# Turning the router's matmul around in two sorted expert stages: the weights stand still, the rows move, and the logits are turned back

## The chip, the core and the metric

The kernel runs on one core of a Trainium2 chip. The metric is the device time in microseconds (us) of one execution, the median of several. TensorE (PE, and PEld for its weight loads) has two clock levels, 1.2 and 2.4 GHz; the profile gives the granted level of a stretch as 0.50 or 1.00.

## The reference, cut to what matters

A stack of eight layers works on `x` (8 batches of 256 rows of 256 numbers). Two of them are mixtures of experts, each of which first computes logits of a router for every row, then picks two experts for a row from them:

```python
# layer 0: 16 experts
scores = xf @ gate_w.T
scores = jax.nn.softmax(scores.astype(jnp.float32), axis=-1)
...
_, idx = jax.lax.top_k(scores, TOPK)
# layer 1: 8 experts
logits = jnp.einsum('bsd,de->bse', x, gate_w) + gate_b
scores = jax.nn.softmax(logits, axis=-1)
topk_s, topk_i = jax.lax.top_k(scores, K)
```

Here `xf` and `x` are the layer's normalised rows: 2048 rows of 256. The router's weights are 256 x 16 in layer 0 and 256 x 8 in layer 1.

## The kernel before, in words

The program is a list of stages, `a0, f0, a1, f1, a2, f2, a3, f3`; each is a block of its own, and no engine begins a stage before all have ended the one ahead (the sequencer rows of L143 are that seam). The stages of interest are `f0` (`sorted_gated_experts`, E = 16) and `f1` (`sorted_experts`, E = 8). Both start in the same way.

VectorE normalises the 16 tiles of 128 rows (L2340 in f0, L2690 in f1) and tells TensorE after every second tile, that is after every batch b. TensorE turns a batch with four transposes of 128 x 128 (`transpose_xn`, L329) into one of two PSUM banks `GP`. ScalarE copies the turned batch to `xnT` in SBUF (L2200, L2616), which later matmuls need too. One step behind, TensorE computes the logits of the batch (L2252, L2649): for each of its 2 tiles and each of the 2 halves of the 256 features, a tile of `xnT` (128 x 128) is loaded as the stationary side and the router's weights, 16 or 8 columns, move:

```python
for t in range((b - 1) * TT, b * TT):
    for k in range(KD):
        op = pe.matmul(logits[:, t * E:(t + 1) * E], xnT[:, k, t * P:(t + 1) * P], wr[:, k, :],
                       start=(k == 0), stop=(k == KD - 1))
```

A float32 matmul of the program stands in the trace as two matmuls with two weight loads, a transpose as one of each; so a batch has 8 pairs for its logits and 4 for its transposes. The logits of all 16 tiles come to lie in one PSUM bank, rows on the partitions (`LG` in f0, `YB[0]` in f1).

When the last is in, `logits_full` lets VectorE go on (L2348 in f0, L2697 in f1): softmax with one exponential on ScalarE (L2202, L2618), the choice of two experts, counts of rows for each expert (two matmuls on TensorE, L2279 and L2280 in f0, L2656 and L2657 in f1), and from these the place of each row in a table sorted by expert. GpSimd then scatters the rows to DRAM with indirect DMAs (L2187, 32 of them; L2603, 16), SyncE fetches them back tile by tile (L2171, L2592), and TensorE starts on the experts (L2298, L2663). In f0 TensorE, ScalarE, GpSimd and VectorE also compute shared experts for all rows meanwhile (L2262 and L2269, L2208 to L2214, L2135 and L2138), in a loop over batches. SyncE zeroes the table (L2162, L2580) and, in f0, loads all experts' weights (L2165) behind that.

Of the kernel before, what the change touches and what calls it, by code (L numbers as in the profile page):

```python
# [17 lines left out]
ACT = mybir.ActivationFunctionType  # L18
AX = mybir.AxisListType

P = 128
B, S, D = 8, 256, 256
TT = S // P
KD = D // P
# [330 lines left out]
def at_least(eng, sem, count):  # L355
    if count > 0:
        eng.wait_ge(sem, count)
# [1688 lines left out]
def sorted_gated_experts(nc, g, name, w):  # L2046
# [9 lines left out]
    E, G, SH = 16, 4, 2  # L2056
# [5 lines left out]
    with ExitStack() as ctx:  # L2062
        sb = lambda n, s, t=F32: ctx.enter_context(nc.sbuf_tensor(f"{name}_sb_{n}", s, t))
        sems, from_one = [], []

        def sem(n, one=False):

            s = ctx.enter_context(nc.semaphore(f"{name}_{n}"))
            (from_one if one else sems).append(s)
            return s  # L2070
        x_slots = nc.dram_tensor(f"{name}_x_slots", (NS * P, D), F32).ap()
        y_slots = g.y_slots[0] = nc.dram_tensor(f"{name}_y_slots", (NS * P, D), F32).ap()
        wr, br = sb("wr", [P, KD, E]), sb("br", [P, E])
# [12 lines left out]
        xnT = sb("xnT", [P, KD, B * S])  # L2086
# [13 lines left out]
        s_y = sb("s_y", [P, TT, D])  # L2100
# [3 lines left out]
        ps = lambda n: ctx.enter_context(nc.psum_tensor(f"{name}_{n}", [P, 2, S], F32))  # L2104
        GP, HB, YB = [ps("gp0"), ps("gp1")], [ps("hb0"), ps("hb1")], [ps("yb0"), ps("yb1")]
        HT = LG, CT = ps("lg"), ps("ct")

        router_in, shared_in, experts_in = sem("router_in"), sem("shared_in"), sem("experts_in")
        sqrt_in, sqrt_out, fixed, cleared = sem("sqrt_in"), sem("sqrt_out"), sem("fixed"), sem("cleared")
        xn_ready, xn_turned, xnT_ready = sem("xn_ready"), sem("xn_turned"), sem("xnT_ready")  # L2110
        logits_full, shifted, exp_ready = sem("logits_full"), sem("shifted"), sem("exp_ready")
        both_ready, counted, routed = sem("both_ready"), sem("counted"), sem("routed")
        s_full = [sem(f"s_full{e}") for e in range(SH)]
# [81 lines left out]
        @block.scalar  # L2195
        def _(act):
            norm_sqrt(act, g, sqrt_in, sqrt_out)
            for b in range(B):
                act.wait_ge(xn_turned, b + 1)
                act.activation(xnT[:, :, b * S:(b + 1) * S], GP[b % 2][:], ACT.Copy).then_inc(xnT_ready, 1)  # L2200
            act.wait_ge(shifted, 1)
            act.activation(ex[:], lg[:], ACT.Exp).then_inc(exp_ready, 1)  # L2202
            act.wait_ge(shared_in, 16 * 5)
            with act.Fori(0, B) as b:
                for e in range(SH):
                    act.wait_ge(s_full[e], b + 1)
                    act.wait_ge(s_product[e], b + 1)
                    act.activation(s_act[:, e], HB[e][:, 0], ACT.Silu, bias=bs1[:, e:e + 1])  # L2208
                    act.activation(s_lin[:, e], HB[e][:, 1], ACT.Identity, bias=bs3[:, e:e + 1])\
                       .then_inc(s_evacuated[e], 1)  # L2210
                act.wait_ge(s_y_full, b + 2)
                act.wait_ge(s_y_added, b + 1)
                for t in range(TT):
                    op = act.activation(s_y[:, t], YB[t][:, 0], ACT.Copy)  # L2214
                op.then_inc(s_y_copied, 1)

            def work(first, last):
                for what, p in slot_steps(first, last):
                    q = p % PAIRS
                    if what == "turn":  # L2220
                        act.wait_ge(turned[q], nth(p))
                        act.activation(xsT[:, ring(p)], GP[p % 2][:], ACT.Copy).then_inc(xT_ready[q], 1)
                    elif what == "hidden":
                        act.wait_ge(h_biased[q], nth(p))
                        act.activation(hm[:, ring(p)], hb[:, ring(p), 0:P], ACT.Silu).then_inc(h_act[q], 1)
                    elif what == "turn_h":
                        act.wait_ge(hT_full[q], nth(p))
                        act.activation(hmT[:, ring(p)], HT[p % 2][:, 0, :].rearrange("p (j n) -> p j n", n=P), ACT.Copy)\
                           .then_inc(hT_ready[q], 1)
                    elif what == "out":  # L2230
                        act.wait_ge(y_ready[q], nth(p))
                        act.dma_start(slots(y_slots, p), ys[:, ring(p), :]).then_inc(y_stored[q], 16)

            work(0, ALWAYS)
            with last_turn(act):
                work(ALWAYS, ALL)

        @block.tensor
        def _(pe):
            pe.wait_ge(router_in, 16 * 6)  # L2240
            logits = LG[:].rearrange("p a n -> p (a n)")
            for b in range(B + 1):
                if b < B:
                    pe.wait_ge(xn_ready, b + 1)
                    if b >= 2:
                        pe.wait_ge(xnT_ready, b - 1)
                    transpose_xn(pe, g, xn[:, b * TT:(b + 1) * TT, :], GP[b % 2]).then_inc(xn_turned, 1)
                if b:
                    pe.wait_ge(xnT_ready, b)
                    for t in range((b - 1) * TT, b * TT):  # L2250
                        for k in range(KD):
                            op = pe.matmul(logits[:, t * E:(t + 1) * E], xnT[:, k, t * P:(t + 1) * P], wr[:, k, :],  # L2252
                                           start=(k == 0), stop=(k == KD - 1))
            op.then_inc(logits_full, 1)
            pe.wait_ge(shared_in, 16 * 5)

# [220 lines left out]
def sorted_experts(nc, g, name, w):  # L2477
# [8 lines left out]
    E, F = 8, 1024  # L2486
# [4 lines left out]
    with ExitStack() as ctx:  # L2491
        sb = lambda n, s, t=F32: ctx.enter_context(nc.sbuf_tensor(f"{name}_sb_{n}", s, t))
        sems, from_one = [], []

        def sem(n, one=False):

            s = ctx.enter_context(nc.semaphore(f"{name}_{n}"))
            (from_one if one else sems).append(s)
            return s
        x_slots = nc.dram_tensor(f"{name}_x_slots", (NS * P, D), F32).ap()  # L2500
        y_slots = g.y_slots[1] = nc.dram_tensor(f"{name}_y_slots", (NS * P, D), F32).ap()
        wr = sb("wr", [P, KD, E])
# [6 lines left out]
        xnT = sb("xnT", [P, KD, B * S])  # L2509
# [26 lines left out]
        GP = [ctx.enter_context(nc.psum_tensor(f"{name}_gp{i}", [P, 2, S], F32)) for i in range(2)]  # L2536
        HB = [[ctx.enter_context(nc.psum_tensor(f"{name}_hb{j}{i}", [P, FC // 2, P], F32)) for i in range(2)]
              for j in range(2)]
        YB = [ctx.enter_context(nc.psum_tensor(f"{name}_yb{j}", [P, 2, S], F32)) for j in range(2)]

        weights_in, sqrt_in, sqrt_out = sem("weights_in"), sem("sqrt_in"), sem("sqrt_out")
        fixed, cleared = sem("fixed"), sem("cleared")
        xn_ready, xn_turned, xnT_ready = sem("xn_ready"), sem("xn_turned"), sem("xnT_ready")
        logits_full = sem("logits_full")
        shifted, exp_ready = sem("shifted"), sem("exp_ready")
        win_ready, counted = sem("win_ready"), sem("counted")
        slots_known, rows_ready = sem("slots_known"), sem("rows_ready")
# [63 lines left out]
        @block.scalar  # L2611
        def _(act):
            norm_sqrt(act, g, sqrt_in, sqrt_out)
            for b in range(B):
                act.wait_ge(xn_turned, b + 1)
                act.activation(xnT[:, :, b * S:(b + 1) * S], GP[b % 2][:], ACT.Copy).then_inc(xnT_ready, 1)  # L2616
            act.wait_ge(shifted, 1)
            act.activation(sc[:], lg[:], ACT.Exp).then_inc(exp_ready, 1)  # L2618
            def turn(i):
                for pair in ((0, 1), (2, 3)):  # L2620
                    for j in pair:
                        act.wait_ge(turned[j], i + 2)
                        act.activation(xsT[:, j], GP[j % 2][:, :, 0:P], ACT.Copy).then_inc(xT_ready[j], 1)  # L2623
                    for j in pair:
                        act.wait_ge(h_full[j], i + 1)
                        for c in range(FC // 2):
                            op = act.activation(hT[:, j, c, :], HB[j % 2][0][:, c, :], ACT.Relu, bias=b1(j, c))
                        op.then_inc(h_act[j], 1)
                    for j in pair:
                        act.wait_ge(y_ready[j], i + 2)  # L2630
                        act.dma_start(y_slots[bass.ds((U * i + j) * P, P), :], ys[:, j, :]).then_inc(y_stored[j], 16)

            run_turns(act, turn)

        @block.tensor
        def _(pe):
            pe.wait_ge(weights_in, 16 * 7)
            logits = YB[0][:].rearrange("p a n -> p (a n)")
            for b in range(B + 1):
                if b < B:  # L2640
                    pe.wait_ge(xn_ready, b + 1)
                    if b >= 2:
                        pe.wait_ge(xnT_ready, b - 1)
                    transpose_xn(pe, g, rows[:, b * TT:(b + 1) * TT, :], GP[b % 2]).then_inc(xn_turned, 1)
                if b:
                    pe.wait_ge(xnT_ready, b)
                    for t in range((b - 1) * TT, b * TT):
                        for k in range(KD):
                            op = pe.matmul(logits[:, t * E:(t + 1) * E], xnT[:, k, t * P:(t + 1) * P], wr[:, k, :],  # L2649
                                           start=(k == 0), stop=(k == KD - 1))  # L2650
            op.then_inc(logits_full, 1)

            pe.wait_ge(win_ready, 1)
# [321 lines left out]
```

## Time and profile before

| what | us |
|---|---|
| median of 3 executions | 1894.47 |
| lowest, highest | 1890.64, 1900.73 |
| the profiled execution, its own time | 1900.78 |
| its span | 1899.0 |
| PE busy (share of the span) | 1516.8 (80%) |
| PEld busy | 1188.3 (63%) |
| DVE (VectorE) busy | 963.4 (51%) |
| ACT (ScalarE) busy | 688.9 (36%) |
| POOL (GpSimd) busy | 493.3 (26%) |

The span is cut in stages with different limits, so the shares say little about one of them. Stage f0 runs from about 227 us of the span, f1 from about 669 us. A busy time of PE tells that matmuls are in flight, not that the array is at its peak: the weight loads (PEld) or the clock can set the pace. All times below are of the profiled execution, in us from the start of its span.

### The profile page before, as it was taken

How to read it: one execution, taken by the hardware profiler on the slowest of the kernel's cores; microseconds unless marked ns; L12 is line 12 of the kernel's file. 1: busy time of each engine (PE TensorE's matmuls, PEld its weight loads, DVE VectorE, ACT ScalarE, POOL GpSimd, SP SyncE). 2: the span in 40 equal slices, each digit the busy share in tenths (PEclk: the TensorE clock that was granted, in tenths of full speed). 3: DMA queues.
4: the chain of work that ended last, by engine and by line, in shares of the span. 5: the costliest groups of instructions: out<-in, count | busy, mean ns of one | idle time of the engine just before them, and what ended most of it. 6: DMA issues, size and time to landing. Idle time of an engine off the chain costs nothing. (4 is left out here: it accounts for less than half of the span.)

```text
span 1899.0 us, 34141 instructions
## 1 busy us (share of the span) xinstructions
PE 1516.8 (80%) x12506; PEld 1188.3 (63%) x12506; DVE 963.4 (51%) x1962; ACT 688.9 (36%) x1527; POOL 493.3 (26%) x833
## 2 busy tenths in 40 slices
PE   3898684865878842999458999997699999999876
PEld 2565473754656542888336666664378888888765
DVE  2676352446645541111456677776326655555652
ACT  1565333321544410111126656665342323332121
POOL 2210027016534303000411355540032323332110
PEclk8899778886889855999769999998799999999986
DMA  5331192446644226886466645452120000000001
GB/s 137 80 77 39 50 351 80 144 139 155 158 109 107 56 83 244 312 313 221 133 155 135 143 104 115 113 114 47 37 73 7 7 7 2 7 7 2 2 7 45
DMA packets 89772, 195.51 MB, mean 103 GB/s; under 512 B 14000, under 2 KB 62512, under 8 KB 81040
## 3 DMA queue, kind: packets, MB, share of 16 engines
q1 hardware_dynamic: 76688, 172.97, 32.2%
q0 software_dynamic: 4608, 12.59, 2.1%
q10 hardware_dynamic: 8320, 7.87, 1.2%
q8 instruction: 98, 1.61, 0.4%
q14 instruction: 58, 0.48, 0.1%
HBM read 136.37 MB, written 57.02 MB: 102 GB/s over the span
## 5 line engine op out<-in xcount | busy, mean ns | idle before, releaser
L987 DVE TENSOR_REDUCE a_sb_mx<-a_mx 128x4 f32<-128x1024 f32 x192 | 234.7, 1222 | 116.6 <-PE a_mx L809 114.0
L730 ACT ACTIVATE a_sb_probs<-a_ex 128x512 f32<-128x512 f32 x384 | 208.8, 598 | 154.7 <-PE a_ex L830 154.3
L1349 DVE RECIPROCAL a_sb_rden<-a_ot 128x256 f32<-128x256 f32 x64 | 112.0, 1750 | 99.4 <-PE a_ot L1233 99.4
L830 PE MATMUL a_ex<-a_sb_QP,a_sb_KP 49*128 49x256 f32 x768 | 99.5, 336 | 32.6 <-ACT a_sb_probs L730 25.9
L266 POOL DMA_INDIRECT a_sb_landing<-f_y_slots,g_pos x48 | 46.6, 970 | 277.6 <-POOLq L143 264.2
L830 PEld LDWEIGHTS a_ex<-a_sb_QP,a_sb_KP 49*128 49x128 f32 x768 | 61.3, 192 | 87.6 <-issue 57.2
L809 PE MATMUL a_mx<-a_sb_KP,a_sb_QP 48*128 48x256 f32 x768 | 89.5, 310 | 33.1 <-DVE a_sb_mx L987 21.2
L843 PE MATMUL a_ot<-a_sb_probs,a_sb_v 128*32 128x256 f32 x1536 | 109.2, 404 | 2.1 <-ACT a_sb_probs L730 2.1
L809 PEld LDWEIGHTS a_mx<-a_sb_KP,a_sb_QP 48*128 48x128 f32 x768 | 62.9, 197 | 45.6 <-DVE a_sb_mx L987 25.5
L1135 POOL TENSOR_TENSOR a_sb_q_lo<-a_sb_whole,a_sb_q_hi 128x512 fp32r<-128x512 f32 x32 | 40.6, 1269 | 172.6 <-ACT a_sb_q_hi L1164 172.6
L2670 PE MATMUL f_hb<-f_sb_xsT,f_sb_wb 128*128 128x128 f32 x640 | 75.2, 279 | 10.9 <-ACT f_sb_xsT L2623 10.9
L1163 ACT ACTIVATE a_sb_whole<-a_gp 128x512 f32<-128x512 f32 x64 | 38.3, 598 | 124.8 <-PE a_gp L1182 124.7
L624 POOL TENSOR_TENSOR a_sb_qs<-a_sb_qf,a_sb_qs 128x512 fp32r<-128x512 f32 x24 | 30.6, 1277 | 203.3 <-ACT a_sb_qs L688 107.5
L1173 ACT ACTIVATE a_sb_probs<-a_sc 128x512 f32<-128x512 f32 x64 | 38.3, 598 | 123.0 <-PE a_sc L1221 85.7
L2670 PEld LDWEIGHTS f_hb<-f_sb_xsT,f_sb_wb 128*128 128x128 f32 x640 | 73.5, 195 | 13.1 <-issue 6.6
L1142 POOL TENSOR_SCALAR_AFFINE_SELECT a_sb_probs<-a_sb_probs 128x256 f32<-128x256 f32 x128 | 49.2, 409 | 120.4 <-ACT a_sb_probs L1174 120.2
L1534 POOL TENSOR_SCALAR_AFFINE_SELECT a_sb_sim<-a_sb_sim 128x256 f32<-128x256 f32 x128 | 51.6, 431 | 98.1 <-ACT a_sb_sim L1589 98.1
L2784 DVE TENSOR_SCALAR f_sb_hT<-f_hb,f_sb_wb 128x128 f32<-128x128 f32 x80 | 22.5, 344 | 104.3 <-PE f_hb L2670 104.3
L2679 PE MATMUL f_yb<-f_sb_wb,f_sb_hT 128*128 128x256 f32 x320 | 70.7, 379 | 0.0
L843 PEld LDWEIGHTS a_ot<-a_sb_probs,a_sb_v 128*32 128x32 f32 x1536 | 41.3, 112 | 38.3 <-issue 12.1
L1334 DVE TENSOR_REDUCE a_sb_mx<-a_sc 128x2 f32<-128x256 f32 (+1 forms) x128 | 61.9, 544 | 6.5 <-PE a_sc L1206 6.4
L2679 PEld LDWEIGHTS f_yb<-f_sb_wb,f_sb_hT 128*128 128x128 f32 x320 | 60.0, 190 | 7.7
(414 smaller groups left out, 3554.2 us busy)
## 6 DMA issues: line engine op xcount, KB each, us to landing
f_sb_wb<-f_w SPq DMA_DIRECT2D x20, 2052.0 KB, 10.2
a_q_moved<-a_sb_qs SPq DMA_DIRECT2D x24, 512.0 KB, 6.1
a_sb_QP<-a_q_moved SPq DMA_DIRECT2D x48, 256.0 KB, 4.0
a_sb_kvT<-ctxT SPq DMA_DIRECT2D x32, 256.0 KB, 3.4
a_k_moved<-a_sb_ks SPq DMA_DIRECT2D x16, 512.0 KB, 4.2
a_sb_KP<-a_k_moved SPq DMA_DIRECT2D x32, 256.0 KB, 5.6
a_sb_QP<-a_q_moved SPq DMA_DIRECT2D x48, 128.0 KB, 4.5
f_x_slots<-f_sb_zero SPq DMA_DIRECT2D x1, 6144.0 KB, 20.0
```

The source lines that it names most:

```text
L266: pool.indirect_dma_start(self.rows[:, b, i, t, :], None, g.y_slots[self.layer], bass.IndirectOffsetOnAxis(g.pos[self.layer][:, i, b * TT ...
L730: act.activation(probs[:, group % 3, 2 * (u % 2) + par], EX[par][:], ACT.Exp, scale=scale)\
L809: op = pe.matmul(MX[:, par, t, :], QP[at:at + R, b % 3, u, t * P:(t + 1) * P], KP[at:at + R, b % KB, u % KM, :], start=True, stop=True)
L830: op = pe.matmul(EX[par][:, t, :], KP[at:at + R + 1, b % KB, u % KM, t * P:(t + 1) * P], QP[at:at + R + 1, b % 3, u, :], start=True, stop= ...
L843: op = pe.matmul(OT[c // 2][32 * j:32 * j + 32, c % 2, :], v4[:, b % 4, t, (4 * c + j) % VH, :], probs[:, (4 * b + c) % 3, j, t, :], start ...
L987: dve.tensor_reduce(pair, MX[:], AX.X, ALU.max, negate=True).then_inc(mx_read, 1)
L1142: op = pool.affine_select(later, later, [[0, 2], [1, P]], ALU.is_ge, 0.0, base=0, channel_multiplier=-1)
L1334: op = dve.tensor_reduce(mx[:, t, 2 * i:2 * i + 2], SC[pair][:, :, t, 0:(t + 1) * P], AX.X, ALU.max, negate=True)
L1349: dve.reciprocal(rden[:, n], OT[n][:, 1, :])
L1534: op = pool.affine_select(later, later, [[0, 2], [1, P]], ALU.is_ge, 0.0, base=0, channel_multiplier=-1)
L2670: op = pe.matmul(HB[j % 2][c // (FC // 2)][:, c % (FC // 2), :], w1(j, k, c), xsT[:, j, k, :], start=(k == 0), stop=(k == KD - 1))
L2679: op = pe.matmul(YB[j % 2][:, 0], hT[:, j, c, :], w2(j, c), start=(c == 0), stop=(c == FC - 1))
```

## The change

In both stages the logits of a batch are computed the other way round. The router's weights (128 x 16 or 128 x 8, for each half of the features) are the stationary side, and the 256 turned rows of the batch move. The result is the logits of the batch turned, 16 or 8 partitions x 256 columns, in a PSUM bank `LT` (two of them in turn, parts of `HB`). ScalarE copies it to `lgT` in SBUF (two buffers; in f0 16 partitions of `s_y`, in f1 a new tile), and TensorE turns it back with two transposes, with the 16 x 16 or 8 x 8 corner of the identity moving, into the place of the logits of before. The three pieces are staggered: in step b TensorE turns batch b, multiplies batch b-1 and turns back the logits of batch b-2. What follows `logits_full` is the same.

```diff
@@ ScalarE, f0 (f1 alike)
-            for b in range(B):
-                act.wait_ge(xn_turned, b + 1)
-                act.activation(xnT[:, :, b * S:(b + 1) * S], GP[b % 2][:], ACT.Copy).then_inc(xnT_ready, 1)
+            for b in range(B + 1):
+                if b < B:
+                    act.wait_ge(xn_turned, b + 1)
+                    act.activation(xnT[:, :, b * S:(b + 1) * S], GP[b % 2][:], ACT.Copy).then_inc(xnT_ready, 1)
+                if b:
+                    act.wait_ge(lgT_full, b)
+                    act.activation(lgT[:, (b - 1) % 2], LT[(b - 1) % 2], ACT.Copy).then_inc(lgT_copied, 1)
@@ TensorE, f0 (f1 alike, with rows for xn)
-            for b in range(B + 1):
+            for b in range(B + 2):
                 if b < B:
                     pe.wait_ge(xn_ready, b + 1)
                     if b >= 2:
                         pe.wait_ge(xnT_ready, b - 1)
                     transpose_xn(pe, g, xn[:, b * TT:(b + 1) * TT, :], GP[b % 2]).then_inc(xn_turned, 1)
-                if b:
+                if 1 <= b <= B:
                     pe.wait_ge(xnT_ready, b)
-                    for t in range((b - 1) * TT, b * TT):
-                        for k in range(KD):
-                            op = pe.matmul(logits[:, t * E:(t + 1) * E], xnT[:, k, t * P:(t + 1) * P], wr[:, k, :],
-                                           start=(k == 0), stop=(k == KD - 1))
+                    at_least(pe, lgT_copied, b - 2)
+                    for k in range(KD):
+                        op = pe.matmul(LT[(b - 1) % 2], wr[:, k, :], xnT[:, k, (b - 1) * S:b * S], start=(k == 0), stop=(k == KD - 1))
+                    op.then_inc(lgT_full, 1)
+                if b >= 2:
+                    pe.wait_ge(lgT_copied, b - 1)
+                    for t in range(TT):
+                        i = (b - 2) * TT + t
+                        op = pe.transpose(logits[:, i * E:(i + 1) * E], lgT[:, b % 2, t * P:(t + 1) * P], g.ident[0:E, 0:E])
             op.then_inc(logits_full, 1)
```

On TensorE, at the start of stage f0, the order of instructions changes like this (L2252 is the logits before; L2258 the turned logits and L2264 their turning back; x4 and x2 count matmuls of the program):

```order
 L329 MATMUL f_gp<-g_ident,f_sb_xn 128x128 x8
-L2252 MATMUL f_lg<-f_sb_wr,f_sb_xnT 128x16 x4
+L2258 MATMUL f_hb<-f_sb_xnT,f_sb_wr 16x256 x2
 L329 MATMUL f_gp<-g_ident,f_sb_xn 128x128 x4
-L2252 MATMUL f_lg<-f_sb_wr,f_sb_xnT 128x16 x4
+L2258 MATMUL f_hb<-f_sb_xnT,f_sb_wr 16x256 x2
+L2264 MATMUL f_lg<-g_ident,f_sb_s_y 128x16 x2
```

Two matmuls with 256 moving columns have come for four with 16, and two transposes have been added; the transposes of the rows stay where they were. At the end of the same stretch on TensorE, ahead of the shared experts:

```order
-L2252 MATMUL f_lg<-f_sb_wr,f_sb_xnT 128x16 x8
-L2273 UNCONDITIONAL_BRANCH
+L2258 MATMUL f_hb<-f_sb_xnT,f_sb_wr 16x256 x2
+L2264 MATMUL f_lg<-g_ident,f_sb_s_y 128x16 x2
+L2258 MATMUL f_hb<-f_sb_xnT,f_sb_wr 16x256 x2
+L2264 MATMUL f_lg<-g_ident,f_sb_s_y 128x16 x4
```

The last two transposes need the copy of the last batch's turned logits. On ScalarE, in stage f1, this stands before:

```order
444 L2616 ACTIVATE f_sb_xnT<-f_gp 128x2x256 x8
445 L2618 ACT_TABLE_LOAD
446 L2618 ACTIVATE f_sb_sc<-f_sb_lg 128x128
```

and this, at the same place, in the changed kernel (its first and last rows; between them the pair of one L2630 and one L2633 repeats):

```order
457 L2630 ACTIVATE f_sb_xnT<-f_gp 128x2x256 x2
458 L2633 ACTIVATE f_sb_lgT<-f_hb 8x256
459 L2630 ACTIVATE f_sb_xnT<-f_gp 128x2x256
```

```order
470 L2633 ACTIVATE f_sb_lgT<-f_hb 8x256 x2
471 L2635 ACT_TABLE_LOAD
472 L2635 ACTIVATE f_sb_sc<-f_sb_lg 128x128
```

Eight small copies have come between and behind the eight large ones, and the load of the exponential's table now stands behind the last of them.

## Rows read from the trace of the kernel before

**Rows 1.** The page's first line

```profile
span 1899.0 us, 34141 instructions
```

**Rows 2.** Busy time by engine (PE, PEld, DVE, ACT, POOL), granted clock, DMA

```profile
233.28:251.70 18.42, 18.42 (x90) 18.42 (x90) 2.00 (x7) 5.46 (x8) 0.00 (x0) 0.50 1.06 356
676.20:694.60 18.40, 18.32 (x89) 18.20 (x88) 1.49 (x5) 5.46 (x8) 0.00 (x0) 0.50 0.44 155
```

**Rows 3.** Timeline of one batch in f0: start, us, what

```profile
237.25 0.90 PEld L329 LDWEIGHTS f_gp<-g_ident,f_sb_xn 128*128 128x128 f32 x4
238.14 1.83 PEld L2252 LDWEIGHTS f_lg<-f_sb_wr,f_sb_xnT 128*128 128x128 f32 x8
238.59 0.60 ACT L2200 ACTIVATE f_sb_xnT<-f_gp 128x512 f32<-128x512 f32 x1 [1.86 <-PE f_gp L329]
...
239.70 0.90 PEld L329 LDWEIGHTS f_gp<-g_ident,f_sb_xn 128*128 128x128 f32 x4
```

**Rows 4.** Timeline of f0: first logits, ScalarE's table, who takes the logits

```profile
233.28 1.78 PEld L2252 LDWEIGHTS f_lg<-f_sb_wr,f_sb_xnT 128*128 128x128 f32 x8 [0.23 <-ACT f_sb_xnT L2200]
...
249.02 1.28 ACT L2202 ACT_TABLE_LOAD   x1
...
251.72 0.43 DVE L2348 TENSOR_REDUCE f_sb_red<-f_lg 128x16 f32<-128x256 f32 x1 [16.44 <-PE f_lg L2252]
...
252.68 0.42 ACT L2202 ACTIVATE f_sb_ex<-f_sb_lg 128x256 f32<-128x256 f32 x1 [2.37 <-DVE f_sb_lg L2350]
```

**Rows 5.** Timeline of f0: counts, places known, scatter

```profile
269.41 1.22 PE L2279 MATMUL f_ct<-f_sb_both,f_sb_before_p 128*128 128x256 f32 x2 [3.15 <-DVE f_sb_both L2380]
...
288.17 0.19 DVE L2433 CAST f_sb_slot<-f_sb_slotf 128x48 int32<-128x48 f32 x1
...
289.62 1.23 POOL L2187 DMA_INDIRECT f_x_slots<-f_sb_xn,g_pos  x1 [2.74 <-issue]
```

**Rows 6.** Timeline of f1: who takes the logits, first expert

```profile
694.63 0.29 DVE L2697 TENSOR_TENSOR f_sb_lg<-f_yb,f_sb_br 128x128 f32<-128x128 f32 x1 [16.93 <-PE f_yb L2649]
...
738.24 0.69 PE L2663 MATMUL f_gp<-g_ident,f_sb_xs 128*128 128x128 f32 x2 [33.33 <-DMA f_sb_xs<-f_x_slots]
```

**Rows 7.** Groups by line in 252.5:254.9, 279:281.8, 344.2:347 (busy us, mean ns)

```profile
L2262 PE MATMUL f_hb<-f_sb_xnT,f_sb_ws 128*128 x7 | 3.2, 634 | 0.0
...
L2262 PE MATMUL f_hb<-f_sb_xnT,f_sb_ws 128*128 x14 | 3.2, 379 | 0.0
...
L2298 PE MATMUL f_gp<-g_ident,f_sb_xs 128*128 128x128 f32 x4 | 0.6, 272 | 0.0
```

**Rows 8.** A ScalarE line: duration ns min/median/max

```profile
L2228 ACT ACTIVATE f_sb_hmT<-f_lg x10: 367/367/367, 349.0 to 406.7; 128x256 f32<-128x256 f32 x10
```

**Rows 9.** Clock around a rise at 251.44: windows as in rows 2

```profile
251.44:255.30 3.86, 3.86 (x10) 3.14 (x11) 2.73 (x8) 1.76 (x3) 0.00 (x0) 0.50 1.04 302
255.50:258.80 3.30, 2.67 (x12) 1.73 (x10) 2.42 (x9) 1.41 (x4) 1.45 (x2) 1.00 0.95 401
```

**Rows 10.** Attention stage a2: windows around a rise, and PE's timeline in the first

```profile
1320.40:1323.70 3.30, 3.28 (x26) 1.71 (x26) 1.71 (x2) 1.38 (x3) 0.00 (x0) 0.50 0.04 10
1323.80:1327.10 3.30, 3.14 (x35) 2.50 (x31) 1.67 (x5) 2.17 (x5) 0.00 (x0) 1.00 0.01 2
...
1320.42 0.79 PE L830 MATMUL a_ex<-a_sb_QP,a_sb_KP 49*128 49x256 f32 x4 [0.84 <-ACT a_sb_probs L730]
...
1321.66 0.59 PE L818 MATMUL a_gp<-g_ident,a_sb_mx 128*8 128x128 f32 x2
1322.18 1.83 PE L843 MATMUL a_ot<-a_sb_probs,a_sb_v 128*32 128x256 f32 x16
```

**Rows 11.** f0's experts start: PE's timeline, and windows around the rise

```profile
339.14 1.08 PE L2298 MATMUL f_gp<-g_ident,f_sb_xs 128*128 128x128 f32 x4 [30.27 <-DMA f_sb_xs<-f_x_slots]
...
340.70:344.00 3.30, 2.98 (x9) 2.24 (x10) 0.00 (x0) 0.75 (x2) 0.00 (x0) 0.50 0.77 224
344.20:347.00 2.80, 2.80 (x17) 2.38 (x16) 1.18 (x3) 0.90 (x2) 0.00 (x0) 1.00 0.14 27
```

**Rows 12.** Window of f0 behind the weights' DMAs

```profile
280.00:285.00 5.00, 4.39 (x20) 3.23 (x19) 5.00 (x44) 2.32 (x6) 2.24 (x3) 1.00 0.03 11
```

More of the change, by code:

```diff
@@ L2106, in sorted_gated_experts @@
         HT = LG, CT = ps("lg"), ps("ct")
+        lgT, LT = s_y[0:E], [HB[i][0:E, 0, :] for i in range(2)]
         router_in, shared_in, experts_in = sem("router_in"), sem("shared_in"), sem("experts_in")
@@ L2110, in sorted_gated_experts @@
         xn_ready, xn_turned, xnT_ready = sem("xn_ready"), sem("xn_turned"), sem("xnT_ready")
+        lgT_full, lgT_copied = sem("lgT_full"), sem("lgT_copied")
         logits_full, shifted, exp_ready = sem("logits_full"), sem("shifted"), sem("exp_ready")
@@ L2539, in sorted_experts @@
         YB = [ctx.enter_context(nc.psum_tensor(f"{name}_yb{j}", [P, 2, S], F32)) for j in range(2)]
+        lgT = sb("lgT", [E, 2, S])
+        LT = [HB[j][0][0:E].rearrange("p c n -> p (c n)")[:, 0:S] for j in range(2)]
         weights_in, sqrt_in, sqrt_out = sem("weights_in"), sem("sqrt_in"), sem("sqrt_out")
@@ L2543, in sorted_experts @@
         xn_ready, xn_turned, xnT_ready = sem("xn_ready"), sem("xn_turned"), sem("xnT_ready")
-        logits_full = sem("logits_full")
+        logits_full, lgT_full, lgT_copied = sem("logits_full"), sem("lgT_full"), sem("lgT_copied")
         shifted, exp_ready = sem("shifted"), sem("exp_ready")
@@ L2613, in _ @@
             norm_sqrt(act, g, sqrt_in, sqrt_out)
-            for b in range(B):
-                act.wait_ge(xn_turned, b + 1)
-                act.activation(xnT[:, :, b * S:(b + 1) * S], GP[b % 2][:], ACT.Copy).then_inc(xnT_ready, 1)
+            for b in range(B + 1):
+                if b < B:
+                    act.wait_ge(xn_turned, b + 1)
+                    act.activation(xnT[:, :, b * S:(b + 1) * S], GP[b % 2][:], ACT.Copy).then_inc(xnT_ready, 1)
+                if b:
+                    act.wait_ge(lgT_full, b)
+                    act.activation(lgT[:, (b - 1) % 2], LT[(b - 1) % 2], ACT.Copy).then_inc(lgT_copied, 1)
             act.wait_ge(shifted, 1)
@@ L2638, in _ @@
             logits = YB[0][:].rearrange("p a n -> p (a n)")
-            for b in range(B + 1):
+            for b in range(B + 2):
                 if b < B:
@@ L2644, in _ @@
                     transpose_xn(pe, g, rows[:, b * TT:(b + 1) * TT, :], GP[b % 2]).then_inc(xn_turned, 1)
-                if b:
+                if 1 <= b <= B:
                     pe.wait_ge(xnT_ready, b)
[L2647 to L2650, printed above, removed]
+                    at_least(pe, lgT_copied, b - 2)
+                    for k in range(KD):
+                        op = pe.matmul(LT[(b - 1) % 2], wr[:, k, :], xnT[:, k, (b - 1) * S:b * S], start=(k == 0), stop=(k == KD - 1))
+                    op.then_inc(lgT_full, 1)
+                if b >= 2:
+                    pe.wait_ge(lgT_copied, b - 1)
+                    for t in range(TT):
+                        i = (b - 2) * TT + t
+                        op = pe.transpose(logits[:, i * E:(i + 1) * E], lgT[:, b % 2, t * P:(t + 1) * P], g.ident[0:E, 0:E])
             op.then_inc(logits_full, 1)
```

## The prediction

> **What bounds the kernel now.** The program is a chain of stages with a seam between them, so I read the two stages that change and no average. The windows come first. In the stretch of the logits, f0 233.28 to 251.70 and f1 676.20 to 694.60, PE and PEld are both busy all the time, and the granted clock is 0.50: the engine works without a break and is yet held at 1.2 GHz [rows 2]. What it does there is loads. One batch, in the timeline, takes 239.70 - 237.25 = 2.45 us: 0.89 for the four loads of the transposes, 1.56 for the eight loads of the logits. A load of 128 columns therefore costs 0.20 to 0.22 us at this level, and the 16 moving columns behind it are hidden [rows 3].
>
> Next, who waits. VectorE had been idle for 16.44 us in f0 and 16.93 us in f1 until the logits were there [rows 4, 6]. From there one chain goes on without slack: VectorE's routing until 288.17, then GpSimd's scatter from 289.62 in f0 [rows 5]; in f1 the same until TensorE, idle 33.33 us, gets its first tile at 738.24 [rows 6]. TensorE's counts in the middle come after an idle of 3.15 us until VectorE was ready [rows 5], so the shared experts do not set the pace there. A microsecond less until `logits_full` is a microsecond less of the stage, in both.
>
> **The change, part by part.** It removes 8 loads with 8 narrow matmuls a batch (1.56 us). It adds 4 matmuls of 256 moving columns with short loads (2 of the program, two each in the trace), 2 loads of 128 columns with narrow matmuls (the turning back), and a copy on ScalarE.
>
> Prices at 1.2 GHz. The nearest row for a wide matmul is the shared experts' just behind: 7 in 3.2 us, each 0.634 long, so a start every (3.2 - 0.634)/6 = 0.428 us [rows 7]. Its stationary side is 128 columns where the new one has 16 or 8; the narrow-sided matmuls of rows 10 run as long, so I take no discount. 4 x 0.43 = 1.71. The two new loads cost 0.21 each, of which the first can go on under the last wide matmul: 0.2 to 0.4. With the 0.89 of the transposes a batch is 2.8 to 3.0, say 2.95 us, against 2.45. At this level the change loses.
>
> Prices at 2.4 GHz. Wide: (3.2 - 0.379)/13 = 0.217, so 0.87 for four. Transposes: 4 in 0.6 us, each 0.272 long, one every 0.11, so 0.44 [rows 7]; the new loads 0.1 to 0.2. A batch is 1.5 us. So the clock decides, and it is the step of this prediction that I am least sure of.
>
> What the clock did after what: in f0 it stayed at 0.50 while TensorE alternated loads and narrow matmuls, and rose at about 255.4, 4.0 us after it had begun on matmuls with 256 moving columns at 251.44 [rows 9]. Full-width weights were not needed for that: in a2 the engine did, ahead of a rise at 1323.8, matmuls with 49 rows, with 32 stationary columns and with 8 (L818, a transpose with 128 moving columns), hardly one that fills the array, and the clock went to 1.00 [rows 10]. Those of 32 columns stand side by side in the array, though, while the new ones stand alone; that is the gap in the evidence. After the change TensorE's time is mostly transposes of rows (128 moving columns) and matmuls of 256, with only the 0.2 to 0.4 us of turning back in 2.95 us without wide movement. I take it that the clock rises.
>
> A rule of the Trainium skill speaks against this. The page "TensorE: Matmul & The Clock Gate", section "Part 4: PE-mode transpose", says that the full clock does not engage for transposes, since they do not count as busy in the same way. Row first: in f0's experts TensorE began at 339.14 with four transposes after an idle of 30 us, was busy for 2.98 of the 3.30 us from 340.7 with nine more matmuls, the next batch's transposes among them, and the clock was up at 344.2 [rows 11]. The trace leans against that rule, but does not refute it. If it held and kept the level at 0.50, the sum would be that of the first rival below instead of the forecast's.
>
> When it rises: in the two rises above it took 4.0 us from the first wide matmul and about 5 from the first transpose [rows 9, 11]. The first transpose of f0 comes 1.8 us ahead of the first logits at 233.28, so the rise should come 2.2 to 3.2 us behind 233.28; I take 2.7, with 1 and 4.4 as the ends. Work from 233.28 to the end of the last wide matmul, at the low level: 2 x 1.71 + 6 x 2.95 = 21.1 us. Of this 2.7 pass at 1.2 GHz, and the other 18.4 take 9.2, with 0.217 in place of 0.214 rather 9.35. That is 245.3. A tail follows that was not there before: the last copy waits for the matmul (its length 0.379 less the 0.217, so 0.16, and some hundredths), takes 0.37 [rows 8], TensorE's two loads, the end of the narrow matmul and VectorE's start some 0.6 more: 1.25 us, of which the turning back of batch 6 hides nothing, since it runs beside the copy. VectorE starts at 246.6 instead of 251.72: **5.1 us less in f0**. f1 has the same counts, and only 8 in place of 16 columns, which neither load nor stream pays for: **5.1 us less**.
>
> What costs nothing, and its cover. ScalarE's work for a batch becomes 0.60 + 0.37 = 0.97 us beside 1.5 on TensorE; without that cover TensorE would wait for `GP` or `lgT`. The stagger gives each copy a step of TensorE. The table load of the exponential (1.28 us) now follows the last small copy: it ends near 247.2, and the exponential is wanted 0.96 behind VectorE's start, at 247.5 [rows 4]; a cover of only 0.3 us, and each tenth beyond it would be a tenth of the stage. Queued behind ScalarE's new wait `lgT_full` is the next large copy, and TensorE needs that one a step later. SyncE's and GpSimd's queues are not touched. The experts' weights in f0 have landed by 280 (DMA 0.03 busy from then) [rows 12], and the scatter would start at 284.5 instead of 289.6, so it meets no traffic.
>
> Sum: -10.2 us. The profiled execution took 1900.78 for a span of 1899.0 [rows 1], 6.3 above the median of the three; it would take 1890.6, and the median 1894.47 - 10.2 = **1884.3 us**, or -0.54%.
>
> **The rivals.** *The clock stays at 0.50* (slower): matmuls that use 8 or 16 columns of the array, with transposes, do not release it. For it speaks that the same stretch is held at 0.50 now although fully busy [rows 2], and that no row has such a narrow matmul alone for long; against it rows 10. The last wide matmul would then end at 233.28 + 21.1 = 254.4, VectorE would start at 255.85: +4.1 in each stage, +8.3 in all, 1902.7 us (+0.44%). It decides by one number: gain and loss meet if the rise comes about 13 us behind the first logits, at 246 in f0; later than that the change loses. Chance 0.11.
>
> *Half a gain*: the clock rises late, or falls back in a stretch, or rises in one stage alone. Each microsecond of delay costs 0.5 a stage. About -5 us, 1889.4. Chance 0.08.
>
> *The gain is met by another wait*: ScalarE's table, the scatter, or the exchange of ScalarE and TensorE at 1.5 us a step. For it speaks the small cover above, against it that all else in the chain moves along; f1 has nothing beside the chain that could meet it. Also about -5, 1889. Chance 0.05. The forecast has 0.76.
>
> **How the numbers follow.** A rise 1.7 us early or late in both stages gives -8.5 to -12; the three executions spread by -3.8 and +6.3 around their median, their median by some 3. The range goes from 1894.47 - 12 - 4 = 1878.5 up to 1893.5, which takes in the two half gains with their scatter and leaves out the slower rival and the tails. About 0.5% (9.5 us) is what a measurement of this kernel can tell from no change. The forecast lies just beyond it: of its 0.76, 0.49 is faster by more than that and 0.27 within; the half gains are within; of the slower rival, 0.44% off, a third or so lands above 0.5%. Faster 0.50, same 0.45, slower 0.05.
>
> **What would show it.** In the changed profile: clock 0.50 at the start of the stretch and 1.00 from about 236 in f0 and 679 in f1; batches 2.95 us apart before and 1.5 after; L2258 every 0.43, then every 0.217 us; VectorE's wait for the logits 11.3 us in f0 in place of 16.44; the scatter 5 us nearer to the stage's start. Wrong would be the prediction with a clock of 0.50 to the end of the stretch, with idle time on TensorE for `f_sb_lgT` in the steps other than the last, or with wide matmuls on 16 columns that cost other than on 128.

## The result, and the profile after

The changed kernel takes 1890.09 us (median of 20 executions, 1880.35 to 1897.49) against 1896.62 us for the kernel before beside it (20 executions, 1889.27 to 1900.75). The ratio is 0.9964, with a 95% interval of 0.9949 to 0.9978: 0.36% faster, inside the 0.5% that a measurement of this kernel can tell from no change. The forecast was 1884.3 us, worked out from a median of 1894.47 us for the kernel before.

The windows of the logits stretch, ahead of the rise of the clock and behind it, first f0 and then f1 (columns as in [rows 2]):

```profile
233.60:238.90 5.30, 5.26 (x18) 2.93 (x19) 3.88 (x13) 1.96 (x4) 0.00 (x0) 0.50 1.01 336
239.00:250.50 11.50, 11.26 (x64) 5.58 (x61) 0.00 (x0) 6.02 (x14) 0.00 (x0) 1.00 1.06 364
673.80:679.20 5.40, 5.37 (x18) 2.90 (x19) 3.41 (x11) 2.08 (x4) 0.00 (x0) 0.50 1.09 386
679.30:690.70 11.40, 11.12 (x63) 5.40 (x61) 0.00 (x0) 5.95 (x13) 0.00 (x0) 1.00 0.35 124
```

Where [rows 2] had one level of 0.50 from end to end, there is now 1.00 over two thirds of the stretch, and PEld is busy for half of the time only.

The timeline of f0, TensorE, from the first transpose on, with two whole batches behind the rise:

```profile
233.64 1.97 PE L329 MATMUL f_gp<-g_ident,f_sb_xn 128*128 128x128 f32 x8 [7.04 <-DVE f_sb_xn L2351]
235.54 1.89 PE L2258 MATMUL f_hb<-f_sb_xnT,f_sb_wr 128*16 128x256 f32 x4
237.36 1.11 PE L329 MATMUL f_gp<-g_ident,f_sb_xn 128*128 128x128 f32 x4
...
239.85 0.65 PE L329 MATMUL f_gp<-g_ident,f_sb_xn 128*128 128x128 f32 x4
240.44 1.04 PE L2258 MATMUL f_hb<-f_sb_xnT,f_sb_wr 128*16 128x256 f32 x4
241.40 0.29 PE L2264 MATMUL f_lg<-g_ident,f_sb_s_y 16*128 16x16 f32 x2
241.63 0.66 PE L329 MATMUL f_gp<-g_ident,f_sb_xn 128*128 128x128 f32 x4
...
243.40 0.66 PE L329 MATMUL f_gp<-g_ident,f_sb_xn 128*128 128x128 f32 x4
```

```profile
241.40 0.20 PEld L2264 LDWEIGHTS f_lg<-g_ident,f_sb_s_y 16*128 16x128 f32 x2 [0.42 <-issue]
241.62 0.42 PEld L329 LDWEIGHTS f_gp<-g_ident,f_sb_xn 128*128 128x128 f32 x4
242.21 0.54 PEld L2258 LDWEIGHTS f_hb<-f_sb_xnT,f_sb_wr 128*16 128x16 f32 x4 [0.17 <-issue]
```

The first load of each new tile shape starts when its matmul's turn has come, and not under the matmul before it.

The end of the stretch in f0, ScalarE, then VectorE, and the scatter; then who takes the logits in f1, and its first expert (these answer to [rows 4], [rows 5] and [rows 6]):

```profile
249.80 0.37 ACT L2206 ACTIVATE f_sb_s_y<-f_hb 16x256 f32<-16x256 f32 x1 [0.82 <-PE f_hb L2258]
250.19 1.28 ACT L2208 ACT_TABLE_LOAD   x1
251.60 0.42 ACT L2208 ACTIVATE f_sb_ex<-f_sb_lg 128x256 f32<-128x256 f32 x1
...
250.64 0.42 DVE L2359 TENSOR_REDUCE f_sb_red<-f_lg 128x16 f32<-128x256 f32 x1 [13.15 <-PE f_lg L2264]
...
288.03 1.23 POOL L2189 DMA_INDIRECT f_x_slots<-f_sb_xn,g_pos  x1 [1.56 <-issue]
...
690.78 0.29 DVE L2719 TENSOR_TENSOR f_sb_lg<-f_yb,f_sb_br 128x128 f32<-128x128 f32 x1 [13.56 <-PE f_yb L2672]
...
734.49 0.69 PE L2685 MATMUL f_gp<-g_ident,f_sb_xs 128*128 128x128 f32 x2 [33.42 <-DMA f_sb_xs<-f_x_slots]
```

The stage is measured from its first transpose, since what lies ahead of it shifts by some us between executions. Before, the first transposes began at these times:

```profile
231.48 1.97 PE L329 MATMUL f_gp<-g_ident,f_sb_xn 128*128 128x128 f32 x8 [7.07 <-DMA f_sb_steps<-c_steps]
674.41 1.97 PE L329 MATMUL f_gp<-g_ident,f_sb_rows 128*128 128x128 f32 x8 [8.34 <-DMA f_sb_steps<-c_steps]
```

VectorE took the logits 20.24 and 20.22 us later ([rows 4], [rows 6]); after, it was 250.64 - 233.64 = 17.00 in f0 and, from 673.83 on, 16.95 in f1. That is 3.24 + 3.27 = 6.5 us, the same as the difference of the medians, whose interval reaches from 4.2 to 9.7 us. Behind the logits nothing changed: to the scatter 37.4 us in place of 37.9 in f0, to f1's first expert tile 43.7 in place of 43.6.

### The profile page after: what moved, and what is told of

Same layout as the page of the kernel before. It is cut to its first block and busy times, and to the rows that moved or that the text cites. A ratio compares the mean times of both kernels' runs of the same rounds, so it can differ in the third digit from the quotient of the medians.

```text
span 1892.1 us, 34104 instructions
## 1 busy us (share of the span) xinstructions
PE 1512.6 (80%) x12474; PEld 1166.8 (62%) x12474; DVE 963.2 (51%) x1962; ACT 694.6 (37%) x1543; POOL 491.5 (26%) x833
```

## The experiments

All are compared by the same three numbers: the batch at full clock, the time of the rise behind the first transpose, and the stage from the first transpose to VectorE's logits. An edit in f0 and f1 is shown once. A negative rise lies ahead of the first transpose. Where the ratio says "one execution", the total was measured once and tells nothing.

| kernel | batch, us | rise f0 / f1, us | stage f0 / f1, us | ratio, 95% interval |
|---|---|---|---|---|
| before | 2.45 (at 0.50) | none | 20.24 / 20.22 | 1 |
| the change | 1.78 | 5.3 / 5.4 | 17.00 / 16.95 | 0.9964 (0.9949 to 0.9978) |
| the change, again | 1.77 | 3.5 / 5.5 | 16.20 / 16.99 | 0.9955 (0.9927 to 0.9983) |
| weights padded | 1.68 | 4.5 / 5.5 | 16.11 / 16.51 | one execution |
| all padded | 1.52 | 4.2 / 5.7 | 15.10 / 15.82 | 0.9970 (0.9947 to 0.9993) |
| fewer waits | 1.78 | 5.3 / 5.5 | 17.00 / 16.98 | 0.9960 (0.9937 to 0.9983) |
| change + warm-up | 1.78 | 1.1 / -1.3 | 15.31 / 14.76 | 0.9943 (0.9917 to 0.9968) |
| all padded + warm-up | 1.52 | 1.3 / -1.4 | 13.90 / 13.50 | 0.9936 (0.9905 to 0.9967) |
| before + warm-up | 1.28 (at 1.00) | 0.7 / -1.5 | 11.74 / 13.01 | 0.9914 (0.9881 to 0.9946) |
| before + warm-up 5, 7 | 1.28 (at 1.00) | 0.7 / -1.4 | 11.74 / 12.92 | 0.9916 (0.9896 to 0.9937) |
| before + 16-column warm-up | 2.45 (at 0.50) | none / none | 20.23 / 20.22 | one execution |
| before + transposes | 2.45 / 1.28 | none / -1.3 | 19.78 / 12.82 | one execution |
| before + 128-column warm-up | 1.28 (at 1.00) | -0.7 / -1.3 | 15.45 / 12.82 | one execution |

The moment of the rise moves from one execution to the next: the change itself had 5.3 us in f0 in one and 3.5 in another, and its stage was 0.8 us shorter for it. So an edit to the batch is read from the batch first, and from the stage only as far as the rise was at the same place.

### What stands between 1.5 and 1.78 us a batch

**Router weights padded.**

```diff
-    op = pe.matmul(LT[(b - 1) % 2], wr[:, k, :], xnT[...], ...)
+    op = pe.matmul(LT[(b - 1) % 2], wrp[:, k, :], xnT[...], ...)   # wrp: wr and zeros, 128 columns
```

> The changed kernel, with the router weights padded by zeros to 128 stationary columns (a copy made by GpSimd in idle time), so that the wide matmuls are 128x256 like the tiles around them; only the 16 or 8 true rows are copied out and turned back. The output is the same. In the changed kernel a batch takes 1.78 us at full clock (f0, 239.85 to 241.62 to 243.40), where ten loads and streams laid end to end by the pitch inside the groups (4 x 0.109 transposes, 4 x 0.216 wide, 2 x 0.109 turning back) give 1.52; the first wide matmul starts 0.20 us behind the last transpose instead of 0.11. Theory A (shape): the next weight load does not go on under the running matmul when the tile's shape changes, and each such seam costs about 0.1 us. It expects the seam from the transposes to the wide matmuls to shrink from 0.20 to 0.11 us and the seam from wide to turning back to stay near 0.31: the batch 1.78 -> 1.68 us, VectorE's start for the logits 0.5 to 0.8 us earlier from the first transpose (17.00 -> 16.3 in f0). Theory B (waits): each group begins with a semaphore wait, and the load waits with it; then nothing moves, 1.78 and 17.0. Clock: if the width of the array that is used matters to the rise, it comes earlier than 5.3 us from the first transpose; if not, at the same 5.3.

Measured, timelines of PE and then of PEld in f0:

```profile
240.66 0.66 PE L329 MATMUL f_gp<-g_ident,f_sb_xn 128*128 128x128 f32 x4
241.15 1.03 PE L2265 MATMUL f_hb<-f_sb_xnT,f_sb_hb 128*128 128x256 f32 x4
242.11 0.29 PE L2271 MATMUL f_lg<-g_ident,f_sb_s_y 16*128 16x16 f32 x2
242.33 0.66 PE L329 MATMUL f_gp<-g_ident,f_sb_xn 128*128 128x128 f32 x4
...
241.04 0.73 PEld L2265 LDWEIGHTS f_hb<-f_sb_xnT,f_sb_hb 128*128 128x128 f32 x4
242.11 0.20 PEld L2271 LDWEIGHTS f_lg<-g_ident,f_sb_s_y 16*128 16x128 f32 x2 [0.33 <-issue]
```

The wide group now begins 241.15 - 240.66 = 0.49 us behind the transposes' (0.59 in the change), its load starts 0.11 ahead of its matmul, and the batch is 1.67 to 1.68. The loads of the turning back, whose tile is still 16 rows high, wait as before. From the last transpose's start to the first wide matmul's it is 0.11 us in place of 0.20. The stage in f0 is 0.9 us shorter, of which about 0.4 is the rise that came 0.8 us earlier; in f1, with the rise at the same place, it is 0.44 us shorter.

**Everything padded.** Also the copy and the turning back on 128 rows:

```diff
-    op = pe.transpose(logits[:, i * E:(i + 1) * E], lgT[0:E][...], g.ident[0:E, 0:E])
+    op = pe.transpose(logits[:, i * E:i * E + P], lgT[...], g.ident[:])
```

> The changed kernel with every tile of the stretch 128x128 on the stationary side: padded router weights, 128 rows of turned logits (112 or 120 of them zeros) copied and turned back with the full identity, 128 moving columns, whose zeros land in columns that the next matmul overwrites. The same output, the same instructions in number and order, the same waits. Theory A (shape change at a seam hinders the load): all three seams go, the batch 1.78 -> about 1.53 us at full clock, the first transpose to VectorE's logits 17.0 -> 15.2 to 15.6 us in both stages, total another -3 us or so to the changed kernel's -6.5: ratio to the kernel before about 0.995. Theory B (the waits at the start of a group): batch stays 1.78, the ratio 0.9965.

```profile
238.07 0.60 PE L329 MATMUL f_gp<-g_ident,f_sb_xn 128*128 128x128 f32 x4
238.51 1.03 PE L2265 MATMUL f_hb<-f_sb_xnT,f_sb_hb 128*128 128x256 f32 x4
239.37 0.38 PE L2271 MATMUL f_lg<-g_ident,f_sb_s_y 128*128 128x128 f32 x2
239.59 0.60 PE L329 MATMUL f_gp<-g_ident,f_sb_xn 128*128 128x128 f32 x4
...
239.16 0.36 PEld L2271 LDWEIGHTS f_lg<-g_ident,f_sb_s_y 128*128 128x128 f32 x2
```

It takes 1.52 us from batch to batch, exactly ten pitches laid end to end (4 x 0.109, 4 x 0.216, 2 x 0.109), with no `<-issue` on PEld; the load of the turning back begins 0.21 us ahead of its matmul. **Fewer waits** on the same tiles as in the change is the rival's run:

```diff
-    if b >= 2:
-        pe.wait_ge(xnT_ready, b - 1)
     transpose_xn(...)
...
-    at_least(pe, lgT_copied, b - 2)
```

> The changed kernel without two of the four waits of a batch on TensorE, those that other waits already imply: xnT_ready for batch b-2 ahead of the transposes, lgT_copied for b-3 ahead of the wide matmuls. Same output, same tiles. Theory B (waits cost the 0.26 us of a batch): the batch goes from 1.78 to about 1.65 us and the stage to 16.2. Theory A (shape): nothing moves: 1.78, 17.0 us, ratio to before as the changed kernel's, 0.996 to 0.997.

```profile
238.36 0.54 PEld L2255 LDWEIGHTS f_hb<-f_sb_xnT,f_sb_wr 128*16 128x16 f32 x4 [0.17 <-issue]
239.33 0.20 PEld L2261 LDWEIGHTS f_lg<-g_ident,f_sb_s_y 16*128 16x128 f32 x2 [0.42 <-issue]
...
239.56 0.66 PE L329 MATMUL f_gp<-g_ident,f_sb_xn 128*128 128x128 f32 x4
...
241.33 0.65 PE L329 MATMUL f_gp<-g_ident,f_sb_xn 128*128 128x128 f32 x4
```

It is still 1.77 to 1.78, with the same idle ahead of the same loads. The kernel has five waits a batch on TensorE and not four, so one was left ahead of each group, and this run alone doesn't clear the waits. The padded one does: with all waits kept and one shape the 0.26 us were gone. So they are the price of three changes of tile shape. It is the change and not the narrow tile's own load: in the lines of the changed kernel the load of the full tile behind the narrow one waited too (241.62 for a matmul at 241.63).

The totals don't show it. All padded measured 0.9970, and its interval, 0.9947 to 0.9993, holds both the 0.995 that was expected and the change's 0.9964. In the four kernels run on that chip (the three above and the change with a warm-up, below) ScalarE stood still for 3 to 17 us at a time in f0's shared experts beside the scatter, and f0's first expert tile came 5.9 us (fewer waits, change + warm-up) or 11.5 to 11.7 us (both padded ones) behind the last scatter, in place of 5.3. From VectorE's logits to that tile f0 took 88.1 and 88.6 us in the two padded kernels and 83.4 and 83.9 in the other two, so in those executions the padding lost more behind the logits than it had won ahead of them. To see whether the edits do that, the change itself was run again, on another chip, with the next kernels.

> The changed kernel as it is, once more, beside the next two. The logits stage is expected as in its first profile: 17.0 us from the first transpose to VectorE's logits in f0 and in f1, ratio 0.9964 within its interval. It is asked for because in the four kernels above, all with unlike logits stages, ScalarE's part of the shared experts stood still for 3 to 17 us at a time while GpSimd's scatter ran in f0, and TensorE's first tile of f0's experts came 6 to 11.5 us behind the last scatter instead of 5.3. If this stall belongs to the program on that occasion and not to the edits, it is here too (at least 6 us and gaps on ScalarE beyond 3 us); if the edits made it, this profile is as the first: 5.3 and no gap.

On this other chip the first expert tile came 5.36 us behind the last scatter, and ScalarE had no such gap beside the scatter; the padded kernel with the warm-up had 5.32, and both took 86.4 us from the logits to that tile. So the padding alone doesn't make the stall, which came with the first chip or the occasion. Why it was longer in the padded kernels stays open, and so does what padding all is worth in the total.

### What the clock costs

**The change with a warm-up**, ahead of TensorE's first wait in the stage, while the norm is being made:

```diff
+    for _ in range(5):
+        pe.matmul(GP[0][:, 0, :], g.ident[:], g.x[:, 0, :], start=True, stop=True)
     pe.wait_ge(router_in, 16 * 6)
```

> The changed kernel with five matmuls of 256 moving columns (identity times the first tile of x, result thrown away) ahead of TensorE's first wait in f0 and in f1, so that TensorE moves columns while the norm of the rows is still being made. In the changed kernel the clock rises 5.3 us behind the first transpose, and those 5.3 us at 1.2 GHz cost about 2.6 us of the stage. If the rise counts from the first movement, wherever it comes from, and the movement joins the transposes without a long gap, the rise comes 1 to 5 us earlier by the stage's marks: first transpose to logits 17.0 -> 14.5 to 16.5, ratio 0.994 to 0.996. If the gap between the warm-up and the first transpose is long, or the rise needs the matmuls of the stage itself, it stays at 17.0 and 0.9965.

The rise came 1.06 us behind the first transpose in f0 and 1.25 ahead of it in f1, 4.2 and 6.7 us earlier than without:

```profile
229.60:230.60 1.00, 1.00 (x6) 1.00 (x6) 1.00 (x4) 0.00 (x0) 0.00 (x0) 0.50 0.87 299
230.70:244.50 13.80, 13.36 (x75) 6.55 (x73) 2.57 (x8) 7.72 (x17) 0.00 (x0) 1.00 1.06 363
660.80:676.60 15.80, 14.56 (x82) 7.13 (x81) 4.44 (x14) 7.97 (x17) 0.00 (x0) 1.00 0.69 242
```

The stages shrank by 1.7 and 2.2 us, and the ratio was 0.9943. With both edits:

> Both edits on the changed kernel: every tile 128 wide (no seams lost, batch 1.52 us) and the warm-up (the clock up within 1 us of the first transpose in f0, before it in f1). The two act on different terms, so they should add: from the first transpose to VectorE's logits 17.0 - 1.7 - 1.7 = 13.6 us in f0 and 17.0 - 2.2 - 1.5 = 13.3 in f1, some 6.6 us less than the changed kernel over both stages if what follows passes it on: ratio 0.992 to 0.994. If f0's shared experts (ScalarE's stalls beside the scatter) end last there, f0's part is lost and it is 0.994 to 0.997.

It took 13.90 and 13.50 us, near the 13.6 and 13.3 expected: the two terms add. The ratio was 0.9936.

**The kernel before with the same warm-up** was meant as the control that gains nothing.

> The kernel before with the same five wide matmuls ahead of TensorE's first wait in f0 and f1: the old loads-and-narrow-matmuls stage, given a higher clock at its start. If the level, once high, were kept by a busy engine whatever it does, the old batch of 2.45 us would be 1.23, and the old stage 10 to 11 us instead of 20.24: far better than the change, ratio 0.99. My theory is that the level is kept by moving columns: the old stage is held at 0.50 because its loads move hardly any, so the clock falls back within some 3 to 7 us of the first logits and the stage is 17 to 20 us, ratio 0.997 to 1.001.

My theory fell here. Windows over the high level and behind it in f0, then in f1, and one batch of f0:

```profile
232.20:242.30 10.10, 9.85 (x91) 9.61 (x89) 2.97 (x10) 5.25 (x9) 0.00 (x0) 1.00 1.05 359
242.45:243.20 0.75, 0.75 (x5) 0.75 (x5) 0.00 (x0) 0.56 (x1) 0.00 (x0) 0.50 1.07 369
658.90:669.00 10.10, 9.08 (x80) 8.42 (x79) 4.66 (x15) 4.07 (x7) 0.00 (x0) 1.00 1.05 364
669.10:673.20 4.10, 4.07 (x20) 3.98 (x19) 0.00 (x0) 1.88 (x2) 0.00 (x0) 0.50 0.08 27
...
235.20 0.51 PEld L329 LDWEIGHTS f_gp<-g_ident,f_sb_xn 128*128 128x128 f32 x4
235.67 0.97 PEld L2254 LDWEIGHTS f_lg<-f_sb_wr,f_sb_xnT 128*128 128x128 f32 x8
236.48 0.51 PEld L329 LDWEIGHTS f_gp<-g_ident,f_sb_xn 128*128 128x128 f32 x4
```

The level did fall, but only after 10.2 us, 0.8 us before the logits were there in f0 and 4.2 us before in f1. Until then the old stage, whose pace its loads set, ran at 1.28 us a batch, half a microsecond less than the change at the same clock. The stages took 11.74 and 13.01 us, 15.7 us less than before, from five matmuls whose result is thrown away; the change won 6.5 and 7.3 us in its two profiles. The total agrees without deciding: 0.9914 (0.9881 to 0.9946) beside 0.9955 (0.9927 to 0.9983) for the change on the same chip.

> The kernel before with the warm-up of five wide matmuls in f0 and seven in f1. With five in both, my expectation fell: the level rose 0.7 us behind the first transpose in f0 and 1.5 us ahead of it in f1, stood at 1.00 for 10.2 us each time although loads alone kept TensorE busy by then, and the stages took 11.75 and 13.00 us in place of 20.24 and 20.21; in f1 it fell two batches before the end. Two more matmuls (0.9 us at 1.2 GHz, 0.4 at 2.4) carry wide movement that much nearer to the first transpose, which now waits 0.8 us for a load from memory. If the fall counts from the last wide movement it comes 0.5 to 1 us later and f1 is 12.5 to 13; if it goes by edges that lie where they lie, f1 stays at 13.0 or is 0.3 longer for the later start. Total as with five: ratio 0.990 to 0.993.

Two more in f1 brought 12.92 in place of 13.01, and the level stood for 10.2 us again: it was not carried along by the later movement in this execution. The ratio was 0.9916 (0.9896 to 0.9937). What ends the high level is not shown by these runs.

**What kind of work raises the level** was asked with three other warm-ups on the kernel before, with one execution each.

> The kernel before with ten matmuls of 16 moving columns in place of the five of 256 (20 loads of 128 columns at 0.213 us: the engine is busy for the same 4.3 us, with loads). If the rise needs moving columns, there is none: 0.50 through the logits stages, 20.2 us each. If a busy engine or any matmul ahead of the stage were enough, as in the run with wide ones: 11.7 and 13.0.

> The kernel before with twenty transposes of 128x128 in place of the five wide matmuls (one every 0.213 us at 1.2 GHz, so again 4.3 us, moving columns in half of it). If transposes don't count as activity (the Trainium skill, page TensorE: Matmul & The Clock Gate, section Part 4: PE-mode transpose), the clock stays at 0.50 and the stages at 20.2 us. If only moved columns count, twenty transposes go on to eight of the stage itself, 6 us at half density: the level rises, at about the first transpose or not at all, and does the same as in the next run, whose matmuls have the same shape.

> The kernel before with ten plain matmuls of 128 moving columns (two loads and two passes each, so twenty loads and twenty movements of 128 columns at the pace of the twenty transposes of the run before this one). It is the control to that run: if both raise the level or both leave it, the kind of the operation is not what counts; if this one rises and the transposes don't, it is.

Windows of f1, each from the warm-up's first instruction: the 16-column matmuls and the stage behind them; the transposes up to the rise and behind it; the plain matmuls of 128 columns up to the rise. The row with L2640 is the transposes' in the timeline:

```profile
664.95:669.60 4.65, 4.42 (x20) 4.32 (x20) 3.65 (x18) 1.46 (x2) 0.42 (x2) 0.50 0.34 76
669.72:689.90 20.18, 20.10 (x96) 19.77 (x96) 3.33 (x11) 6.06 (x9) 0.00 (x0) 0.50 0.49 175
```
```profile
663.32:666.70 3.38, 3.38 (x16) 3.38 (x17) 2.39 (x14) 1.46 (x2) 0.41 (x2) 0.51 0.17 24
666.90:677.00 10.10, 9.15 (x84) 8.68 (x83) 4.51 (x14) 4.07 (x7) 0.00 (x0) 1.00 1.05 368
...
663.32 4.04 PE L2640 MATMUL f_gp<-g_ident,g_x_all 128*128 128x128 f32 x20 [3.52 <-PEq L143]
```
```profile
661.02:664.50 3.48, 3.48 (x17) 3.48 (x18) 2.49 (x14) 1.46 (x2) 0.41 (x2) 0.52 0.20 29
```

TensorE was busy nearly without a break in all three. With 16 columns the clock stayed at 0.50 through f1's warm-up and stage, and both stages took 20.2 us. (In f0 the level was still at 1.00 from the stage ahead for 16 of the 20 passes of that warm-up, so only f1 tests it.) With transposes alone it rose at 666.79, 3.5 us behind the first of them, and with plain matmuls of the same shape at 664.56, again 3.5 behind; f1 took 12.8 us in both. The Trainium skill (page "TensorE: Matmul & The Clock Gate", section "Part 4: PE-mode transpose") says that the full clock does not engage for transposes; this trace shows it engaging, so here the measurement decides against the page. In f0 the two differ: the plain matmuls met 0.50, raised the level at 231.07, and it fell at 237.90 (15.45 us); the transposes met a level that still stood at 1.00 from the stage ahead, went through in 2.38 us, TensorE was then idle for 2.01 us, the level fell at 229.89 and did not come back (19.78 us). The 16-column warm-up of f0 met the high level too, and it did not last either. So a warm-up that begins while the level is still up can be spent ahead of the stage; no run here shows how often that happens with the five wide matmuls, which had 0.50 from within 0.2 us of their start in all their profiles.

## Why the prediction was right, and where its size was off

**Who waits for whom**: right. As far as the total can tell (6.5 us, interval 4.2 to 9.7), the stages' 6.5 us came out whole; VectorE's idle time fell from 16.44 to 13.15 us, and the scatter and f1's first tile moved with it.

**The clock rises** (the step I was least sure of): right, in both stages and in each of the six other executions profiled with the new logits. Forecast 2.7 us behind the first logits, with ends at 1 and 4.4; measured 238.95 - 235.54 = 3.4 in f0 and 3.5 in f1. Each microsecond costs half of one: 0.4 us a stage. Part of that is a slip: the 2.7 took the 4.0 us of [rows 9], which count from a first wide matmul, as if they counted from the first transpose. Taken as they stand, the two rows say 4.0 behind the first logits or 3.2, and the measured rise lies between. The slower rival, that a side of 16 or 8 columns keeps the level at 0.50, did not happen; padding it to 128 made no clear difference either (4.5 and 4.2 us behind the first transpose in f0, where the change itself had 5.3 and 3.5 in two profiles; 5.5 and 5.7 against 5.4 and 5.5 in f1).

**The prices of the wide matmuls**: right. Four in 1.89 us at 1.2 GHz with the last one's length in it, a start every 0.42; four in 1.04 at 2.4 GHz, one every 0.22. A narrow stationary side costs what a full one does.

**"A batch is 1.5 us"**: the term that failed. I let the first load of the turning back go on under the last wide matmul and forgot the other two seams; "the new loads 0.1 to 0.2". It measured 1.78 us, because the load of a tile of another shape waited for its turn at each of three seams: 0.20 in place of 0.11 us, 0.31 in place of 0.22, 0.14 in place of 0.11, and 0.05 more inside the group of transposes behind the third (0.38 from its first start to its fourth, where three pitches are 0.33). The padded kernels brought that back to 1.68 and 1.52. Five whole batches at full clock make 5 x 0.28 = 1.4 us, and the one across the rise another 0.2 (2.49 us). Some 0.2 more fell due at the low level (the first batch pair took 3.72 us where 8 transposes and 4 wide matmuls at my prices make 3.5), and the tail was 0.2 shorter than the 1.25 I took (249.60, where four pitches from the last group's start end, to 250.64). With the rise that is 0.4 + 1.4 + 0.2 + 0.2 - 0.2 = 2.0 us, of the 1.9 that are missing in each stage: 5.1 forecast, 3.2 measured.

**ScalarE's table**: right but narrow. It ended at 251.47 and the exponential began at 251.60, 0.96 behind VectorE's start, as before. So no other wait met the gain, and the late rise took 0.4 us a stage of it; what halved it was neither of the two rivals that forecast -5, but the price of a batch.

**Luck**: the measured 1890.09 lies in the range of 1878.5 to 1893.5 because its upper end had been set for half gains of other causes. Of the 5.8 us between forecast and result 3.7 are gain that did not come, and 2.1 are the kernel before, whose median over 20 executions is 1896.62 and not 1894.47.

**What the prediction never asked** is whether the change was needed for the clock. At equal clock it is a loss, 1.78 against 1.28 us a batch; what it earns is the rise, and a level that stood to the end of the stage. The rise can also be had while TensorE is idle, at no cost that these stages show.

## What to carry to other kernels

When a stretch in which TensorE is busy throughout shows 0.50, first ask what ran in the idle time ahead of it: a few matmuls with many moving columns there, on data that is at hand, raised the clock and gave 15.7 us in the two stages where reshaping the work gave 6.5 to 7.3. Look in the profile whether the level was down when the warm-up began. When small products of different shapes take turns on TensorE, count each change of shape as up to 0.1 us at full clock, or pad the tiles to one shape, which here cost neither stream nor load time. And test a layout at the clock it would have anyway, or its gain may be the clock's alone.

## What I had not expected of the hardware

- A level once raised outlasted its cause: with loads and 16 or 8 moving columns for two thirds of the time it stood at 1.00 for 10.2 us in six of seven stages and for 6.8 in the seventh, while the same work never raised it in 18 us.
- Twenty transposes raised it as twenty plain passes of the same shape did, 3.5 us behind the first.
- Padding took no time on TensorE: 128 stationary columns in place of 16, and 128 moving in place of 16 behind a load of 128, had the same pitch (0.217 and 0.109 us), and equal shapes let the next load begin 0.11 to 0.21 us ahead of its matmul.
- On one chip ScalarE stood still for up to 16.7 us beside GpSimd's scatter, although its data were there (in the all-padded kernel it began at 320.23 what TensorE had finished by 306.1); on another the same program did not. The cause is open.
